# Expert tiles in pairs beside the first scan of a two-layer scan and mixture-of-experts block

## The reference, cut to what matters

```
xn = layernorm(x)
x  = x + scan0(xn) + ffn0(xn)

scan0: delta = softplus(xn @ Wd + b)                   # [tokens, 256]
       h_t = exp(delta_t * A) * h_(t-1) + delta_t * x_t * B_t    # per feature and state, 16 states
       y_t = sum over states of h_t * C_t,  plus x_t * D
ffn0:  each token picks 4 of 16 experts; expert: silu(x @ Wg) * (x @ Wu), 176 wide, then @ Wdown
       weighted sum over the 4 experts, plus a shared expert
```

## Time and profile before

| quantity | value |
|---|---|
| median of three runs | 1200.81 us |
| the profiled execution | 1205.48 us, span 1203.7 us |
| PE, DVE, ACT, POOL busy in the span | 81%, 76%, 41%, 36% |
| changed stage, first bx to last hc | 202.06 to 570.16 us |
| read-out, last hc to the last statistics of layer 1's layernorm | 570.16 to 591.00 us |

### The profile page before, as it was taken

One profiled execution on the slowest core, in us unless ns is written; L12 is line 12 of the kernel. 1 busy time (PEld: TensorE's weight loads), 2 busy tenths in 40 slices (PEclk: granted clock), 3 DMA queues, 4 the chain that ended last, 5 costly groups with the idle time before them and its releaser, 6 DMA issues. The chain is left out here.

```text
span 1203.7 us, 18601 instructions
## 1 busy us (share of the span) xinstructions
PE 976.7 (81%) x6048; PEld 578.1 (48%) x6048; DVE 914.1 (76%) x1506; ACT 497.0 (41%) x1130; POOL 434.9 (36%) x332
## 2 busy tenths in 40 slices
PE   3987997788787778773787686889988988899885
PEld 2354555444444444441634353445555555456553
DVE  4659567989999999999657746677677767677676
ACT  2201135554555555543121124545455554554542
POOL 0000100777787877753171010322322232133310
PEclk9989999989999999995798798999998999999998
DMA  6960172787878878878650041443433343244524
GB/s 220 369 172 1 52 164 74 134 155 144 165 148 156 162 149 159 147 141 182 142 148 5 0 99 38 112 95 86 112 87 93 87 106 93 67 95 104 116 40 141
DMA packets 107092, 143.27 MB, mean 119 GB/s; under 512 B 30022, under 2 KB 97334, under 8 KB 102710
## 3 DMA queue, kind: packets, MB, share of 16 engines
q0 software_dynamic: 30368, 77.92, 33.5%
q1 hardware_dynamic: 76630, 64.14, 19.2%
HBM read 72.80 MB, written 39.46 MB: 93 GB/s over the span
## 5 line engine op out<-in xcount | busy, mean ns | idle before, releaser
L1501 POOL DMA_INDIRECT sum<-yo,to_i x48 | 78.0, 1624 | 317.1 <-ACT yo L1459 301.2
L1171 POOL DMA_INDIRECT xg<-xn_d,token_i x80 | 96.2, 1203 | 175.1 <-DVE to_i L460 93.4
L1164 POOL DMA_INDIRECT sum<-yo,to_i x80 | 140.3, 1754 | 46.8 <-DMA sum<-yo,to_i 23.7
L1011 PE MATMUL bank<-areaA,xgT 128*128 x320 | 120.6, 502 | 15.0 <-issue 9.9
L1028 PE MATMUL bank<-areaA,hidT 88*128 x320 | 91.7, 410 | 45.8 <-ACT hidT L1076 41.7
L2048 DVE TENSOR_TENSOR areaD<-areaD,gb 128x512 f32<-128x512 f32 x128 | 87.5, 688 | 53.0 <-ACT areaD L1995 49.2
L1028 PEld LDWEIGHTS bank<-areaA,hidT 88*128 88x128 f32 x320 | 55.6, 193 | 76.7 <-issue 72.1
L686 PE MATMUL bank<-xnT,areaB 128*128 128x512 f32 x192 | 86.8, 599 | 0.8 <-DVE y L716 0.8
L1846 PE MATMUL bank<-xnT,w_in 128*128 128x512 f32 x160 | 85.5, 661 | 2.2 <-ACT ecn L1751 1.5
L1011 PEld LDWEIGHTS bank<-areaA,xgT 128*128 128x128 f32 x320 | 56.8, 196 | 58.0 <-issue 41.5
L1491 POOL DMA_INDIRECT xg<-xn_d,token_i x48 | 53.9, 1123 | 82.6 <-DVE to_i L460 68.2
(11 more groups left out here) (342 smaller groups left out, 2141.6 us busy)
## 6 DMA issues: line engine op xcount, KB each, us to landing
y<-xnT POOLq DMA_DIRECT2D x21, 1024.0 KB
wst<-gu_f SPq DMA_DIRECT2D x96, 176.0 KB
y<-areaB POOLq DMA_DIRECT2D x11, 1024.0 KB
wst<-down_f SPq DMA_DIRECT2D x48, 176.0 KB
areaA<-in_gu SPq DMA_DIRECT2D x2, 2816.0 KB
gu_f<-in_gu POOLq DMA_DIRECT2D x1, 5632.0 KB, 17.0
sum<-yo SPq DMA_DIRECT2D x2, 2176.0 KB, 16.2
down_f<-in_down POOLq DMA_DIRECT2D x1, 2816.0 KB, 22.6
```

The source lines that it names most:

```text
L1011: last = nc.tensor.matmul(bank[:, GB + q % 2, 0:2 * FI], xgT[:, q % 2, k, :], wgu0_of(e, k), start=(k == 0), stop=(k == KD - 1))
L1164: nc.gpsimd.indirect_dma_start(sum0_d[q % 2], bass.IndirectOffsetOnAxis(ap=to_i[:, q:q + 1], axis=0), yo[:, q % 5, :], None, compute_op=AL ...
L1171: nc.gpsimd.indirect_dma_start(xg[:, q % 5, :], None, xn_d[0], bass.IndirectOffsetOnAxis(ap=token_i[:, q:q + 1], axis=0)).then_inc(s.gathe ...
L1501: nc.gpsimd.indirect_dma_start(sum1_d, bass.IndirectOffsetOnAxis(ap=to_i[:, q:q + 1], axis=0), yo[:, q % 4, :], None, compute_op=ALU.add). ...
```

## The change: what it does

The tiles 2m and 2m+1 become an expert pair m of 40, with one tick `silu_tick[m]` = 1 + 249m // 39: 1, 7, 13, 20, ... 237, 243, 250, so a pair every 6.4 ticks. `silu` and `gate_tanh` handle both tiles in one instruction each way, over two banks at once (2x176 elements), and write in place in one of two buffers (`act_t` for even pairs, `hid` for odd ones). Relative to the pair's tick s, the order is now: gate_up of the next pair at s+1 and s+2; hid_transposes of the first tile at s+2; down of the first tile, tanh of the next pair and x_transposes of tile 2m+4 at s+3; hid_transposes of the second tile at s+4; down of it and x_transposes of tile 2m+5 at s+5. The last down is at tick 255. `gate_up` of a later pair now waits for the silu of the pair before (`hid_ready`), whose banks it overwrites. GpSimd's program, the scan's instructions and the read-out are unchanged.

```diff
+        silu_tick = [1 + (TICKS0 - 7) * m // (PAIRS0 - 1) for m in range(PAIRS0)]
+        rows_of = (act_t, hid)
+        def tile_at(t, ahead, at):
+            if t - at not in silu_tick:
+                return None
+            q = 2 * silu_tick.index(t - at) + ahead
+            return q if q < NT0 else None
...
         def gate_up(pe, q):
             pe.wait_ge(s.xT_ready, q + 1)
+            if q > 1:
+                pe.wait_ge(s.hid_ready, q // 2)
...
         def hid_transposes(pe, q):
-            pe.wait_ge(s.hid_ready, q + 1)
+            pe.wait_ge(s.hid_ready, q // 2 + 1)
...
         def layer0_tensor(pe):
-            x_transposes(pe, 0)
-            gate_up(pe, 0)
-            x_transposes(pe, 1)
+            for q in range(2):
+                x_transposes(pe, q)
+                gate_up(pe, q)
+            for q in range(2, 4):
+                x_transposes(pe, q)
...
-                if part == 1 and q < NT0:
-                    hid_transposes(pe, q)
-                if part == 1 and q + 2 < NT0:
-                    x_transposes(pe, q + 2)
-                if part == 0 and q + 1 < NT0:
-                    gate_up(pe, q + 1)
-                if part == 2 and q < NT0:
-                    down(pe, q)
+                for step, ahead, at in ((gate_up, 2, 1), (gate_up, 3, 2), (hid_transposes, 0, 2), (down, 0, 3), (x_transposes, 4, 3),
+                                        (hid_transposes, 1, 4), (down, 1, 5), (x_transposes, 5, 5)):
+                    q = tile_at(t, ahead, at)
+                    if q is not None:
+                        step(pe, q)
...
         def gate_tanh(act, q):
-            act.wait_ge(s.gu_full, q + 1)
-            nc.scalar.activation(act_t[:, q % 2, :], bank[:, GB + q % 2, 0:FI], ACT.Tanh, scale=0.5).then_inc(s.tanh_ready, 1)
+            act.wait_ge(s.gu_full, q + 2)
+            nc.scalar.activation(rows_of[q // 2 % 2][:, :, :], bank[:, GB:GB + 2, 0:FI], ACT.Tanh, scale=0.5).then_inc(s.tanh_ready, 1)
...
         def layer0_scalar(act):
+            xT_copy(act, 1)
             gate_tanh(act, 0)
-            xT_copy(act, 1)
+            for q in range(2, 4):
+                xT_copy(act, q)
...
+                for step, ahead, at in ((hT_copy, 0, 2), (gate_tanh, 2, 3), (y_copy, 0, 3), (xT_copy, 4, 3), (hT_copy, 1, 4), (y_copy, 1, 5),
+                                        (xT_copy, 5, 5)):
...
         def silu(v, q):
-            v.wait_ge(s.tanh_ready, q + 1)
-            first = vec.done(nc.vector.scalar_tensor_tensor(act_t[:, q % 2, :], act_t[:, q % 2, :], 1.0, bank[:, GB + q % 2, 0:FI], ALU.add, ALU.mult))
+            v.wait_ge(s.tanh_ready, q // 2 + 1)
+            z = rows_of[q // 2 % 2][:, :, :]
+            first = vec.done(nc.vector.scalar_tensor_tensor(z, z, 1.0, bank[:, GB:GB + 2, 0:FI], ALU.add, ALU.mult))
             v.wait_ge(vec.sem, first)
-            nc.vector.scalar_tensor_tensor(hid[:, q % 2, :], act_t[:, q % 2, :], 0.5, bank[:, GB + q % 2, FI:2 * FI],
-                                           ALU.mult, ALU.mult).then_inc(s.hid_ready, 1)
+            nc.vector.scalar_tensor_tensor(z, z, 0.5, bank[:, GB:GB + 2, FI:2 * FI], ALU.mult, ALU.mult).then_inc(s.hid_ready, 1)
...
         def layer0_vector(v):
-                if t == 1:
-                    silu(v, 0)
-                q, part = divmod(t, TILE)
-                if part == 2 and q + 1 < NT0:
-                    silu(v, q + 1)
+                q = tile_at(t, 0, 0)
+                if q is not None:
+                    silu(v, q)
```

More of the change, by code:

```diff
@@ L955, in _program @@
         TICKS0 = UN * UNIT
-        assert TICKS0 >= TILE * (NT0 + 2)
+        PAIRS0 = NT0 // 2
+        assert NT0 % 2 == 0 and TICKS0 >= TILE * (NT0 + 2)
+        silu_tick = [1 + (TICKS0 - 7) * m // (PAIRS0 - 1) for m in range(PAIRS0)]
[5 more added lines that the diff above has]
+            return q if q < NT0 else None
         BROW, CROW, XB, HY, GB = 0, 2, 4, 5, 6
@@ L1019, in hid_transposes @@
             for h in range(2):
-                last = nc.tensor.transpose(bank[0:FH, HY, h * P:(h + 1) * P], hid[:, q % 2, h * FH:(h + 1) * FH], ident[:, :])
+                last = nc.tensor.transpose(bank[0:FH, HY, h * P:(h + 1) * P], rows_of[q // 2 % 2][:, q % 2, h * FH:(h + 1) * FH], ident[:, :])
             last.then_inc(s.hT_full, 1)
@@ L1095, in layer0_scalar @@
             act.wait_ge(delta_ready, 4)
+            xT_copy(act, 1)
             gate_tanh(act, 0)
-            xT_copy(act, 1)
+            for q in range(2, 4):
+                xT_copy(act, q)
             for t in range(TICKS0):
[L1099 to L1107, removed]
+                for step, ahead, at in ((hT_copy, 0, 2), (gate_tanh, 2, 3), (y_copy, 0, 3), (xT_copy, 4, 3), (hT_copy, 1, 4), (y_copy, 1, 5),
+                                        (xT_copy, 5, 5)):
+                    q = tile_at(t, ahead, at)
+                    if q is not None:
+                        step(act, q)
                 if t % UNIT == 0 and t // UNIT + 1 < UN:
```

## The result

The changed kernel takes 1269.47 us (median of 4 runs, 1268.65 to 1274.51) against 1201.93 for the kernel before in the same session (1198.93 to 1206.51): a ratio of 1.0563, 95% interval 1.0530 to 1.0595. The forecast was 1211 us with a range to 1226. The direction is right, the size is not: +68 us instead of +10.

What follows compares the result with a forecast made beforehand. DVE was taken to bound the stage. Silu pairs -6.0, tanh waits -8.7, PE's order +9, POOL's order +5 and the end +11 gave +10.3 us on 1200.8: 1211 us, range 1191 to 1226 us.

Steps and rivals of the forecast that it cites:

- Silu in pairs: DVE in the stage: paired instructions of 352 elements replace two of 176 each, 6.0 us less.
- Waits for the tanh: DVE in the stage: its 14.0 us of tanh waits go except 5.3 us at the start, net 8.7 us less.
- What PE's new order costs: PE in the stage: lost slack makes bx wait for B rows, half clock included; 9 us more, bounds 0 and 23.
- third rival: PE and ACT bound every round in the stage, 9.3 us each: 20 us more, 1221 us; chance 0.20.
- What POOL's unchanged order costs: POOL in the stage: add_scan stands behind later scatters, so DVE waits for adds; 5 us more, bounds 0 and 12.
- What the end costs: After the last hc: late scatters and adds delay reload and read-out; 11 us more, bounds 7 and 16.
- The scan stays the bound: In the stage PE absorbs its new order and adds land in time: faster, 1193 us; chance 0.27.

Runs made afterwards that it cites:

- run with less PE work: Changed kernel without the second half of the down product, so its output is not the reference's: 1260.88 us, ratio 1.0482.
- gate products ahead: Against the early B row kernel, second gate_up moved right behind the first hid_transposes, x_transposes later, next pair's tanh at s+1: 1237.64 us.
- early B row: Changed kernel with PE and ScalarE steps interleaved, pairs every 6 ticks, B row product mostly one tick earlier, first silu at tick 2: 1202.27 us.
- spread kernel before: Kernel before the change, turns of its single tiles stretched from 3 to 3.16 ticks, last down at tick 252, POOL's turns kept: 1237.78 us.
- fillers in the interleaved order: Changed kernel with PE and ScalarE steps interleaved at 6.4 ticks, plus 8 unread transposes ahead of each pair's first gate_up: 1256.34 us, 1265.83 without them.
- fillers in the changed kernel: Changed kernel plus 4 unread transposes per pair between the first hid_transposes and the first down: 1270.50 us, ratio 1.0562.
- two interleaved kernels at 6 ticks: Changed kernel with PE and ScalarE steps interleaved and pairs every 6 ticks: 1202.16 us; the same with the early B row: 1202.27 us.

## Why the prediction was right or wrong

**Silu in pairs: right.** Predicted 0.51 us an instruction and 6.0 us less; measured 0.513 and 0.520, and DVE's busy time in the stage is 5.5 us less. The 10 us that the prediction worked out by the Trainium skill ("VectorE: DVE Perf Modes", TRN2 errata) would have been too much.

**Waits for the tanh: nearly.** The start cost 6.0 us for 5.3. Behind it 3.4 us stayed in 4 places, none of which I had.

**What PE's new order costs: this is the step that failed.** I put it at 9 us with bounds 0 and 23, and the stage by that at 367.4 us (368.1 - 14.7 + 9 + 5). The stage took 411.4, and waits for the B row alone are 31.2. The chain at full clock was not undercounted: I had up to 7 us for it, and the five waits that no half-clock stretch precedes make 3.1 us. The mistake is in "the granted clock of the stage was 0.94, so an eighth of it ran at 1.2 GHz": I took the clock of before as a constant of the kernel and left about 2 us for it. It is a result of PE's order and distances. The change brings it to 0.86 and adds 34.6 us of PE busy time for the same products; at PE's busy share of 0.76 in both kernels that would be 46 us of stage, and 43.3 were measured. That agreement is arithmetic, not proof, and the run with less PE work, whose share is 0.72, doesn't fit it.

What the runs show of the cause: order and distances together. Undoing the distances alone gave back 22 us and left a clock of 0.85, undoing the order alone gave back nothing that can be told from noise and left 0.84, and both undone bring 0.97 and the old time. Distances of 6 and 8 at almost the same mean as 6.4 give 0.95 instead of 0.87, and 20 us. The order with the gate products ahead brings 0.92 down to 0.84 and costs 35 us. The account that fits these, and the seven long waits at half clock, is that the order sets where PE waits, the clock follows, and a low clock makes the next waits longer (1.34 and 3.14 us for two B rows). It isn't shown, since no run holds the order and moves the clock alone, and some runs speak against the clock as the measure of the loss: the early B row has a clock of 0.92 and a stage of 365.7 us, the spread kernel before 0.92 and 383.5, the fillers in the interleaved order 0.93 and 398.5, and the fillers in the changed kernel 0.89 and a stage that is not shorter. My third rival, "PE and ACT become the bound of every round" at 9.3 us, names the place but took the half clock as a shift of every round; in fact the rounds free of half clock last 9.0 us on average and the others 11.0, 397 us for 39 rounds, 10.2 on average.

What stays open: how much of the 43 us is the low clock, and how much is the order at any clock. And which property of an order keeps the clock up I can't say; I forecast 1195 for the gate products ahead and 1192 for the early B row, and missed both.

**What POOL's unchanged order costs: right in kind, too small.** 5 us (0 to 12) forecast, 21.5 measured as waits, in 7 places, all after 500 us, so the late ones of the stage as predicted. Placing POOL's steps by their pair takes them all away and gives 11 us of the stage back. The add alone, which I took at 6.6 us from issue to landing, has a median of 7.9 to 8.3 (32 adds), and y is later by each half-clock stretch; both go into the same sum.

**What the end costs: the mechanism to the point, the price too low.** Forecast: last scatter within 2 us of E, reload at E + 6.7 to 7.5, read-out at E + 14, +11 us (7 to 16). Measured: E + 2.1, E + 8.2, E + 22.1, +19.3. The term that was too cheap is the time from the first reload to the read-out: 7 us in my count (E + 7 to E + 14), 13.9 measured (the earlier trace rows have 13.7 from 559.27 to 572.97, which I had put down to the late add alone). The whole lies above even my upper bound of 16. The Trainium skill ("DMA: Bandwidth & Descriptors", queues, rings and completion order) has the engines take turns between queue rows, from which the prediction worked out that overlapping transfers finish late together. The trace agrees: the add issued at 623.02 landed at 635.6, the reloads issued at 623.24 and 623.67 at 635.7 and 637.0, and the 16 us of that estimate were nearer than my 11. Where POOL's order follows the pairs, the last add had landed (at 611.5) before the reload started at 612.88, and the read-out came 5.6 us behind that start and not 13.9. In the kernels with 6 ticks the reload starts at E - 9.4 to E - 10.8 and the read-out at E + 1.6 to E + 3.2, as before.

**Rivals.** "The scan stays the bound" fell. What it was to give, 1193 us, no run gave: even with the loss removed, the two interleaved kernels at 6 ticks stand at the time of before. Their profiles have the 6 us of the pairs, but DVE's waits are 18.1 and 16.4 us where they were 14.0, and the stages are 1.5 and 2.4 us shorter, less than a run can tell. No kernel here is faster than the one before.

## What to carry to other kernels

The granted clock of TensorE is an outcome of the order in which its work and its waits lie, not a rate to multiply with: where a change reorders the products, forecast one case with the clock kept and one with it lower, and don't let the bounds end where the clock of before would put them. The early B row shows that a lower clock need not come with a longer stage (0.92 instead of 0.97, and 365.7 us instead of 366.6). Read the distances between periodic work of different periods (here 6 or 6.4 ticks against a product every 8 ticks) before spreading anything evenly, since a regular pattern that the kernel has found may be worth more than even spacing. And work moved toward the end of a stage has to be followed through every queue behind it, down to the reload of the next stage: here dealing to the last tick cost 10 to 19 us there.

## What was not expected of the hardware

TensorE's busy share hardly moved. In 80 us stretches of the stage PE was busy 61 to 65 us, about 0.78, in the kernel before, in the changed one and in the one with both edits undone, at clocks from 0.84 to 1.00; what moved is the work done in it, which DVE's busy time shows. The stretch 445 to 525 us of the changed kernel, of the one with both edits undone, and of the one with the leading gate_up:

```profile
445.00:525.00 80.00, 61.15 (x219) 36.77 (x220) 67.33 (x56) 35.27 (x83) 49.35 (x38) 0.89 0.70 130
```
```profile
445.00:525.00 80.00, 63.31 (x252) 36.84 (x251) 71.91 (x59) 41.05 (x100) 62.07 (x44) 0.98 0.84 154
```
```profile
445.00:525.00 80.00, 62.93 (x233) 38.82 (x232) 68.07 (x56) 38.15 (x89) 60.74 (x41) 0.87 0.78 144
```

In these rows the busy share doesn't tell one clock from the other: 0.79 went with 0.98, and 0.79 with 0.87. Nor does the mean length of a wait: those for hidT were 0.48 us on average with both edits undone (28.5 us in 60 places, clock 0.97) and 0.90 with the leading gate_up (35.9 in 40, 0.84), but 0.89 before (41.7 in 47) at 0.94. The kernel with less PE work shows the other side: 58 us busy in the same stretch and a clock of 0.82.
